# A top-1 expert feed-forward: every expert on every token, or 15 gathered tiles of tokens sorted by expert

## The reference, cut to what matters

```python
scores = feats @ centroids.T                      # 1024 x 8
expert = argmax(scores)                           # one expert for each token
alpha = sigmoid(max(scores))
h = layernorm(feats) * gamma[e] + beta[e]         # a second layernorm
ys[e] = feats + relu(h @ W1[e].T + b1[e]) @ W2[e].T + b2[e]
out = alpha * ys[expert] + (1 - alpha) * feats    # = feats + alpha * (relu(...) @ W2.T + b2)
```

## Time and profile before

| | before |
|---|---|
| median of 3 runs | 762.81 us (762.22 to 766.0) |
| the profiled execution's own time | 763.13 us |
| its span | 761.3 us |
| busy: TensorE, VectorE, ScalarE, GpSimd | 700.4, 524.7, 413.2, 237.6 us |
| mean granted TensorE clock, of full | 0.964 |
| chain that ended last, by engine | TensorE 67%, VectorE 15%, issue 6% |

### The profile page before, as it was taken

One profiled execution on the slowest core, in us unless ns is written; L12 is line 12 of the kernel. 1 busy time (PEld: TensorE's weight loads), 2 busy tenths in 40 slices (PEclk: granted clock), 3 DMA queues, 4 the chain that ended last, 5 costly groups with the idle time before them and its releaser, 6 DMA issues.

```text
span 761.3 us, 13863 instructions
## 1 busy us (share of the span) xinstructions
PE 700.4 (92%) x5137; PEld 511.9 (67%) x5137; DVE 524.7 (69%) x1063; ACT 413.2 (54%) x636; POOL 237.6 (31%) x207
## 2 busy tenths in 40 slices
PE   5999888999999999999998999888999998979995
PEld 4655555665666778777777755476667766748884
DVE  6688676687766648688887588888656556724444
ACT  4387552236665550699995277746665553224442
POOL 4000011014364561022223000013575757046742
PEclk9999899999999998699999999999999999779998
DMA  8200000050013020000024500000022020211112
GB/s 341 122 2 1 2 0 1 0 235 2 26 33 86 2 56 1 1 1 0 0 80 158 226 2 1 2 1 2 1 58 60 26 57 1 57 28 34 43 31 89
DMA packets 9760, 35.54 MB, mean 47 GB/s; under 512 B 1535, under 2 KB 5987, under 8 KB 8162
## 3 DMA queue, kind: packets, MB, share of 16 engines
q1 hardware_dynamic: 7170, 31.58, 12.4%
q0 software_dynamic: 1472, 2.59, 1.6%
q10 hardware_dynamic: 1056, 0.52, 0.2%
HBM read 31.94 MB, written 3.20 MB: 46 GB/s over the span
## 4 chain that ended last, share of the span: by engine, by line
PE 67%; DVE 15%; issue 6%; POOL 5%; ACT 5%; DMA 1%; POOLq 0%; SPq 0%; ACTq 0%; DVEq 0%
PE banks L215 7%; PE banks L216 6%; PE banks L217 6%; PE banks L980 5%; PE banks L487 4%; PE banks L545 4%; PE banks L968 3%; PE banks L2026 3%; PE banks L1017 3%; POOL work L1165 3%; DVE work L772 2%; PE banks L1498 2%; PE banks L2016 2%; PE banks L462 2%; PE banks L504 2%
## 5 line engine op out<-in xcount | busy, mean ns | idle before, releaser
L1165 POOL TENSOR_TENSOR work<-work 128x512 f32<-128x512 f32 x64 | 85.4, 1340 | 95.3 <-ACT work L1127 95.2
L772 DVE TENSOR_REDUCE work<-banks 128x2 f32<-128x512 f32 x128 | 84.5, 688 | 24.2 <-PE banks L487 17.8
L304 POOL TENSOR_TENSOR ln_rstd<-ln_var_eps,minus_half_and_newton 128x4 f32<-128x4 f32 x16 | 17.1, 1066 | 165.0 <-DVE ln_var_eps L270 156.3
L980 PE MATMUL banks<-work 128*64 128x256 f32 x512 | 63.9, 388 | 2.6 <-ACT work L1127 2.2
L1810 DVE TENSOR_TENSOR work_split<-work,work_split 128x512 fp32r<-128x512 f32 x64 | 52.0, 814 | 19.1 <-ACT work_split L1732 18.5
L215 PE MATMUL banks<-normed_t_high,work_split 128*128 128x512 f32 x114 | 55.2, 484 | 4.7 <-DVE normed_t_low L353 2.4
L968 PEld LDWEIGHTS banks<-work_split 64*128 64x128 f32 x768 | 47.6, 186 | 12.6 <-issue 7.2
L968 PE MATMUL banks<-work_split 64*128 64x256 f32 x768 | 54.1, 287 | 0.2
L980 PEld LDWEIGHTS banks<-work 128*64 128x64 f32 x512 | 32.9, 136 | 30.2 <-ACT work L1127 13.8
L1227 DVE TENSOR_TENSOR work_split<-banks,work_split 128x512 fp32r<-128x512 f32 x32 | 21.9, 686 | 44.9 <-ACT work_split L1107 44.8
L1127 ACT ACTIVATE work<-work,small_operands 128x1024 f32<-128x1024 f32 x32 | 36.8, 1150 | 28.6 <-DVE work L1239 28.1
(11 more groups left out here) (360 smaller groups left out, 1777.7 us busy)
## 6 DMA issues: line engine op xcount, KB each, us to landing
raw_b<-in_wf SPq DMA_DIRECT2D x1, 6528.0 KB, 19.0
raw_a<-in_wf SPq DMA_DIRECT2D x1, 4096.0 KB, 12.6
raw_b<-reciprocal_rows SPq DMA_DIRECT2D x6, 512.0 KB, 5.5
raw_a<-reciprocal_rows SPq DMA_DIRECT2D x6, 512.0 KB, 5.5
raw_a<-in_wf SPq DMA_DIRECT2D x1, 2048.0 KB, 14.4
raw_b<-in_wb SPq DMA_DIRECT2D x1, 2048.0 KB, 18.8
raw_a<-in_wb SPq DMA_DIRECT2D x1, 2048.0 KB, 8.3
small_operands<-in_small SPq DMA_DIRECT2D x1, 1386.0 KB, 10.2
```

The costliest lines, as they stand in the source:

```text
L772: nc.vector.tensor_reduce(a_nm[:, t:t + 2, j], bank(7 - n % 2).rearrange("p (e k) -> p e k", e=2), AX.X, ALU.max, negate=True).then_inc(A[ ...
L980: last = nc.tensor.matmul(ps[DH * h:DH * (h + 1), 4, (b % 2) * S:(b % 2 + 1) * S], w_v[:, 2 * b + kb, (2 * p + h) * DH:(2 * p + h + 1) * D ...
L1165: nc.gpsimd.tensor_tensor(w_ps[g % 2].rearrange("p (h q) -> p h q", h=2), v[:, :, 0, :], v[:, :, 1, :], ALU.add).then_inc(W["ps"].sem, 1)
```

## The change

The f1 sublayer is rewritten on the pattern of the last one. VectorE computes factors for the second layernorm exactly, ScalarE writes rows (normed token, alpha, index), SP stores them to HBM, and after ranks and slots 15 tiles of 128 slots are gathered (8 + 7, since each expert may leave one tile partly filled; all 15 are always computed). A tile: transpose, a copy scaled by gamma on VectorE, one native f32 matmul of 512 columns on unsplit weights, a copy out of PSUM on VectorE, four transposes, four activations on ScalarE with the bias at an address held in a register, a one-row product that brings b2, four native f32 products, the factor alpha, a scatter. Then SP loads the 1024 rows back, and VectorE adds them (`f1_add`). Register tables of addresses are loaded by `find` on TensorE, ScalarE and VectorE for eight tiles at a time. The pieces, the clears and the copy to `xh` ahead of the sublayer go; SP's later loads of weights now stand behind `f1_rows`; the last feed-forward shares semaphores and small tensors with this one and is otherwise the same. `rank_products`, `first_of_equals` and `expert_starts` are its lines L2036 to L2039, L2197 to L2198 and L2213 to L2218 moved into functions. The diff, cut:

```diff
- G = signals("f1", E // 2, w=10, up=16, a=16, al=16, dn=16, cb=2, cc=2, t=4, acc=4)
+ TILES1 = NT + E - 1
+ TABLE1 = 2 * NT
  s_gb, s_gd = sem("f1_bias_product"), sem("f1_bias_shifted")
- g_w = [(wr[:, 2048 * s:2048 * s + 1024], wr[:, 2048 * s + 1024:2048 * s + 2048]) for s in range(2)]
...
+ rows1_dram = nc.dram_tensor("token_rows", (T + 1, SLOT), F32, kind="Internal").ap()
+ back1_dram = nc.dram_tensor("expert_tokens", (T, D), F32, kind="Internal").ap()
...
+ M = {n: Count("sorted_" + n, t) for n, t in dict(
+     xs=TILES1, xh=0, xl=TILES1, up=TILES1, sg=0, af=TILES1, tr=TILES1, at=TILES1, o=TILES1, y=TILES1).items()}
...
+ slots1 = wf[:, 0:TILES1 * SLOT].rearrange("p (j c) -> p j c", c=SLOT)
+ rows1 = wf[:, 2048:2048 + NT * SLOT].rearrange("p (t c) -> p t c", t=NT)
+ again1 = wf[:, 2048:2048 + T].rearrange("p (t d) -> p t d", t=NT)
+ n_af = [wf[:, 3200 + 512 * k:3712 + 512 * k] for k in range(2)]
+ n_at = [wf[:, 4224 + 512 * k:4736 + 512 * k] for k in range(2)]
...
+ def find(tables, j, tiles, engine, groups):
...
+     for k, (at, most) in groups.items():
+         _, values = nc.values_load_multi_w_load_instructions(
+             tab_t[0:1, at + j:at + j + n], engines=[engine], min_val=0, max_val=most,
...
+         for i in range(n):
+             tables[j + i, k] = values[i]
...
- def f1_shifts_dve(dve):
+ def f1_shifts_dve(dve, order):
      dve.wait_ge(s_gb, 2)
      b1 = col("b1")
      nc.vector.tensor_tensor(b1, b1, ps[:, 5, S:S + E * NF], ALU.add).then_inc(s_gd, 1)
+     nc.vector.tensor_scalar(n_v2, Z[0].mv[:, :, 1], 1.0 + EPS, EPS * EPS, ALU.mult, ALU.add).then_inc(s_v2, 1)
+     order.done(nc.vector.memset(n_ec[:, 0:1], -63.5))
...
+ def f1_pe(pe, m):
+     def at(name, n):
+         M[name].wait(pe, 0, n)
+     where = {}
+     def slot_back(j):
+         loaded_slot(pe, 0, j)
+         at("xl", j)
+         nc.tensor.transpose(ps[:, 7, 0:P], slots1[:, j, 0:D], ident).then_inc(M["xs"].sem, 1)
+     def up(j):
+         find(where, j, TILES1, mybir.EngineType.PE, {
+             "raw": (0, (E - 1) * W_F1), "b2": (2 * TABLE1, (E - 1) * D)})
+         at("af", j - 1)
+         at("xl", j + 1)
+         nc.tensor.matmul(bank(j % 2), n_x[j % 2], raw_a[:, bass.ds(where[j, "raw"], 512)], start=True, stop=True)\
+             .then_inc(M["up"].sem, 1)
+     def turn(j):
+         at("af", j + 1)
+         at("at", j)
+         for f in range(NF):
+             last = nc.tensor.transpose(ps[:, 4, f * P:(f + 1) * P], n_af[j % 2][:, f * P:(f + 1) * P], ident)
+         last.then_inc(M["tr"].sem, 1)
+     def output(j):
+         at("at", j + 1)
+         at("y", j - 1)
+         o = ps[:, 6 - j % 2, 0:D]
+         nc.tensor.matmul(o, const("ones")[0:1, :], sm[0:1, bass.ds(where[j, "b2"] + SMALL["b2rows"][0], D)],
+                          start=True, stop=False)
+         for f in range(NF):
+             last = nc.tensor.matmul(o, n_at[j % 2][:, f * P:(f + 1) * P],
+                                     raw_a[:, bass.ds(where[j, "raw"] + (512 + f * P), P)], start=False, stop=f == NF - 1)
+         last.then_inc(M["o"].sem, 1)
+     logits_pe(xf, col("centroids"), 5, ready=2 * m + 1)
+     stream(8, 4)
+     rank_products(pe, 0)
+     stream(16, 4)
+     pe.wait_ge(s_spots, 1)
+     for t in range(NT):
+         last = nc.tensor.matmul(ps[:, 7, 256:256 + TABLE1], n_spot[:, t, :], n_b[:, t, :], start=t == 0, stop=t == NT - 1)
+     last.then_inc(s_who, 1)
+     stream(8, 4)
+     pe.wait_ge(s_tab, 5)
+     slot_back(0)
+     slot_back(1)
+     up(0)
+     for j in range(TILES1):
+         if j + 2 < TILES1:
+             slot_back(j + 2)
+         if j + 1 < TILES1:
+             up(j + 1)
+         turn(j)
+         if j:
+             output(j - 1)
+     output(TILES1 - 1)
...
+ def f1_act(act):
+     def at(name, n):
+         M[name].wait(act, 0, n)
+     where = {}
+     def hidden(j):
+         find(where, j, TILES1, mybir.EngineType.Activation, {"b1": (3 * TABLE1, (E - 1) * NF)})
+         at("tr", j + 1)
+         at("o", j - 1)
+         for f in range(NF):
+             ins = nc.scalar.activation(n_at[j % 2][:, f * P:(f + 1) * P], ps[:, 4, f * P:(f + 1) * P], ACT.Relu,
+                                        bias=sm[:, bass.ds(where[j, "b1"] + (SMALL["b1"][0] + f), 1)])
+         ins.then_inc(M["at"].sem, 1)
+     act.wait_ge(s_s2, 1)
+     for t in range(NT):
+         nc.scalar.activation(rows1[:, t, 0:D], xn[:, t, :], ACT.Copy, scale=n_t2[:, t:t + 1]).then_inc(s_row2, 1)
+     act.wait_ge(s_lx, 2)
+     nc.scalar.activation(n_ex, mcol, ACT.Exp, scale=-1.0).then_inc(s_le, 1)
+     act.wait_ge(s_gd, 1)
+     act.wait_ge(s_tab, 5)
+     for j in range(TILES1):
+         hidden(j)
...
+ def f1_pool(pool):
+     nc.gpsimd.iota(idx_t[:, :], pattern=[[P, 2 * NT]], base=0, channel_multiplier=1).then_inc(s_index, 1)
+     pool.wait_ge(s_v2, 1)
+     nc.gpsimd.tensor_tensor(n_r2, n_v2, small_cols[:, 0:1].to_broadcast((P, NT)), ALU.pow).then_inc(s_r2, 1)
+     pool.wait_ge(s_index, 1)
+     nc.gpsimd.tensor_copy(rows1[:, :, D + 1].bitcast(I32), idx_t[:, 0:NT]).then_inc(s_index, 1)
+     pool.wait_ge(s_got, 1)
+     pool.wait_ge(s_rows, 16)
+     pool.wait_ge(s_blanked, 32)
+     def fetch(j):
+         nc.gpsimd.indirect_dma_start(
+             out=slots1[:, j, :], out_offset=None, in_=rows1_dram,
+             in_offset=bass.IndirectOffsetOnAxis(ap=who_t[:, j:j + 1], axis=0), bounds_check=T, oob_is_err=False)\
+             .then_inc(s_slot[j % AHEAD], 16)
+     for j in range(AHEAD):
+         fetch(j)
+     for j in range(TILES1):
+         M["y"].wait(pool, 0, j + 1)
+         nc.gpsimd.indirect_dma_start(
+             out=back1_dram, out_offset=bass.IndirectOffsetOnAxis(ap=slots1[:, j, D + 1:D + 2].bitcast(I32), axis=0),
+             in_=slots1[:, j, 0:D], in_offset=None, bounds_check=T - 1, oob_is_err=False).then_inc(s_back, 16)
+         if j + AHEAD < TILES1:
+             fetch(j + AHEAD)
+     pool.wait_ge(s_back, 16 * TILES1)
+ def f1_rows(sp):
+     sp.wait_ge(s_row2, NT)
+     sp.wait_ge(s_index, 2)
+     sp.wait_ge(s_wrow, 1)
+     sp.dma_start(rows1_dram[1:1 + T, :].rearrange("(t p) c -> p t c", p=P), rows1).then_inc(s_rows, 16)
+     sp.wait_ge(s_rows, 16)
+     sp.wait_ge(s_back, 16 * TILES1)
+     for h in range(2):
+         src = back1_dram[h * HALF:(h + 1) * HALF, :].rearrange("(t p) d -> p t d", p=P)
+         sp.dma_start(again1[:, 4 * h:4 * h + 4, :], src).then_inc(s_again[h], 16)
...
+     def second_factors():
+         dve.wait_ge(s_r2, 1)
+         dve.wait_ge(s_v2, 1)
...
+         nc.vector.tensor_tensor(n_t2, n_t2, n_r2, ALU.mult).then_inc(s_s2, 1)
+     def choose():
+         dve.wait_ge(ld["route"], 16)
+         nc.vector.tensor_reduce(mcol, logits, AX.X, ALU.max).then_inc(s_lx, 1)
+         dve.wait_ge(s_lx, 2)
+         order.step(nc.vector.tensor_tensor(t1, logits, across(mcol), ALU.is_equal))
+         first_of_equals(order, m2col)
+         order.step(nc.vector.tensor_tensor(hot, t1, across(m2col), ALU.is_equal))
+         nc.vector.tensor_tensor_scan(prefix, const("seg"), hot_et, 0.0, ALU.mult, ALU.add).then_inc(s_hot, 1)
+     def row_weights():
+         order.step(nc.vector.tensor_scalar(n_ex, n_ex, 1.0, None, ALU.add))
+         nc.vector.reciprocal(rows1[:, :, D], n_ex).then_inc(s_wrow, 1)
+     def place():
+         dve.wait_ge(s_rank, 1)
+         rank = expert_starts(order, n_ct, n_in, n_ec)
...
+         nc.vector.tensor_tensor(n_spot, const("iota").unsqueeze(1).to_broadcast((P, NT, P)),
+                                 across(n_ss, P), ALU.is_equal).then_inc(s_spots, 1)
+     def table():
+         order.step(nc.vector.tensor_tensor(n_le, n_in.unsqueeze(1).to_broadcast((P, TABLE1, E)),
+                                            across(const("tile_at")[:, 0:TABLE1]), ALU.is_le))
+         order.step(nc.vector.tensor_reduce(n_te, n_le, AX.X, ALU.add))
+         for k, width in enumerate((W_F1, 512, D, NF, 1)):
+             nc.vector.tensor_scalar(tab_t[:, k * TABLE1:(k + 1) * TABLE1], n_te, float(E - 1), float(width),
+                                     ALU.min, ALU.mult).then_inc(s_tab, 1)
+     def who():
+         dve.wait_ge(s_who, 1)
+         nc.vector.tensor_copy(who_t[:, 0:TABLE1], ps[:, 7, 256:256 + TABLE1]).then_inc(s_got, 1)
+     def slot(j):
+         find(where, j, TILES1, mybir.EngineType.DVE, {"gamma": (4 * TABLE1, E - 1)})
+         at("xs", j + 1)
+         at("up", j - 1)
+         nc.vector.tensor_scalar(n_x[j % 2], ps[:, 7, 0:P], gamma_at(where, j), None, ALU.mult).then_inc(M["xl"].sem, 1)
+     def evict(j):
+         at("up", j + 1)
+         at("tr", j - 1)
+         nc.vector.tensor_copy(n_af[j % 2], bank(j % 2)).then_inc(M["af"].sem, 1)
+     def out(j):
+         at("o", j + 1)
+         nc.vector.tensor_scalar(slots1[:, j, 0:D], ps[:, 6 - j % 2, 0:D], slots1[:, j, D:D + 1], None, ALU.mult)\
+             .then_inc(M["y"].sem, 1)
+     second_factors()
+     choose()
+     row_weights()
+     place()
+     table()
+     who()
```

(37 more changed lines are left out.)

374 lines of the change are left out of this document (100 added, 274 removed).

## The result

| | before | after |
|---|---|---|
| median of the runs | 764.4 us (4 runs) | 738.4 us (737.02 to 739.36, 4 runs) |
| ratio to before | | 0.9668, 95% interval 0.9628 to 0.9707 |
| the profiled execution's own time, its span | 763.13, 761.3 us | 739.17, 737.4 us |
| busy: TensorE, VectorE, ScalarE, GpSimd | 700.4, 524.7, 413.2, 237.6 us | 665.2, 467.1, 343.6, 244.5 us |
| mean granted TensorE clock, of full | 0.964 | 0.941 |

Faster, by 3.3%: 739.17 us in the profiled execution where 729.6 was forecast.

What follows compares the result with a forecast made beforehand. TensorE was taken to set the pace, its old stage lasting 106.1 us. Head 20.9, loop 38.5, clock 2.5 and tail 7.7 make 69.6, so -36.5, +3 behind: 729 us, range 720 to 740.

Steps and rivals of the forecast that it cites:

- The head: Routing and gather before the first tile's product: 20.9 us, summed from logits, fillings, ranks, slots, rows of slots, gathers and register loads.
- the filling ahead of the slots: In the head, 16 filling products before TensorE's next step after the ranks: 5.0 us taken, between 4.0 and 6.1.
- The loads of 16 registers ahead of the first product: End of the head: register loads behind the second gather, 0.78 us of issue; 1.1 with the transpose.
- the sentence on the one-row product: In each loop tile, the product for b2 was bounded by 0 and 0.22 us; 0.22 was taken.
- The second load of registers: In the loop, TensorE's second load of address registers was to add up to 0.4 us.
- the half clock in mid-loop: Named sign of error: a PEclk of 0.50 in the middle of the tile loop.
- The clock at the loop's head: First tiles: TensorE waits some 4 us for the gather and loses clock; 2.5 us taken, between 0 and 5.4.
- Tail: From the last product through scatter and load back to SBUF: 7.7 us, between 6.7 and 8.65.
- Behind the stage: Normalisation 4 and the small attention begin on a slow TensorE after the idle tail: +3 us, from 0 to 6.
- ScalarE's four activations: Rival: ScalarE paces the loop at 0.60 us per activation, 2.95 us a tile, +6.5 in all: 736 us; chance 0.10.
- the threshold of 4.9 us a tile: Rival: tiles run one after another, some 5.2 us each, 767 us; it decides from 4.9 a tile; chance 0.04.
- the half clock held for one or two tiles, not for 15: Rival: the clock stays at the half level for all tiles, loop costs 38.5 us more, 765 us; chance 0.03.

Runs made afterwards that it cites:

- the identity product: The changed kernel with the second biases brought in by a 128x128 identity against equal rows instead of one row of ones: 730.7 us, ratio 0.9551.

## Why the prediction was right, and where it was off

- *What bounds it*: right. The old stage took 106.1 and 105.5 us, TensorE's, and what was saved in it, 27.4 us, came out of the span but for 1.2 ahead of it and 2.4 behind. The new loop runs at the sum of TensorE's parts.
- *The head*: right in the sum, 20.9 against 21.1, 18.9 and 19.0; the term that moves is the filling ahead of the slots (bounds 4.0 to 6.1, taken as 5.0, measured 5.46 mostly at the half clock, 3.79 at the full one, where VectorE's slots end 0.3 us later). The store of rows held nothing up. The loads of 16 registers ahead of the first product were on the path as forecast: 0.61 us of issue in the chain after VectorE had the tile ready, 0.78 forecast.
- *The loop: the step that failed is the sentence on the one-row product*, "bounded by 0 and the 0.22 of one of the four products". It is 0.61, above the upper bound, since it also changes the price of its neighbours: 0.22 for the columns, 0.19 and 0.20 for the two changes of row count. 15 x 0.39 = 5.9 us. The upper bound was taken from a product of 128 rows, when the trace held products of 32 among products of 128, with the 0.19 to 0.20 behind them; the nearest row was the one with few rows, not the one with the same columns. The other terms of the tile (0.86, 0.44, 0.89, 0.11) came out exact, as the identity product shows.
- *The second load of registers*, "adds up to 0.4", is the other term that was too small: TensorE stood still 1.36 us, and then ran at the half clock for 3.5 to 7 us. The prediction names no row for the 0.4. The trace of before has a stop of 0.45 us at such a load (724.08 to 724.53), but there two loads of 1.07 and 1.10 us lie under 2.0 us of products, here under 1.1. Together stop and half clock cost 3.2 to 4.9 us over three tiles; the half clock in mid-loop, which the prediction named as a sign of being wrong, was no term of the sum, and its cause is not settled.
- *The clock at the loop's head*: right in place, smaller in size as far as filling shows it: it brought 1.2 us of the 2.5 back.
- *Tail*: 7.7 against 8.0. *Behind the stage*: the span behind the addition is 351.0, 346.5 and 351.1 us after, 348.6 and 351.3 before, so that +3 is not shown; the forecast's reason, fills at the half clock, is in the trace (24 records in 5.4 us), but the executions differ by more.
- *The rivals*: ScalarE's four activations take 1.14 us a tile and pace nothing; the tiles overlap (the threshold of 4.9 us a tile, given for them, is 5.0 by its own sum); the half clock held for one or two tiles, not for 15. The rule of the Trainium skill on a burst after a wait, cited in the prediction ("TensorE: Matmul & The Clock Gate", section on HAM oscillation), agrees with the loop's head in this trace (0.57 from 325 to 333 us) and with the stretch behind the tail (0.51 from 386 to 394 us).
- *Luck*: 738.4 lies within 720 to 740 although the loop took 8.6 us more than forecast. The upper end was made of other things, clock, gather, filling and tail, that hardly came; it held the loop's two errors by its width and not by its reasons.

## What to carry to other kernels

A small product is priced with its neighbours: a one-row product between products of 128 rows cost 0.61 us a tile where a full product of the same columns cost 0.22, so a bias is better brought in by the identity against equal rows. Register loads at tile boundaries are better spread over the tiles, since those of eight tiles at once stopped TensorE for 0.8 to 1.9 us, and those of one tile not visibly; in the time that is shown only together with the identity product. And a forecast for a kernel whose clock moves needs a second profile of before: here the stretch ahead of the change came out at 306.6 and 309.3 us.

## What was not expected of the hardware

A change in the number of rows between two products cost 0.19 to 0.20 us each way at the full clock, with the weight loads standing still for 0.12 to 0.17 us there. The granted clock fell to its lower level for 3.4 us (a mean of 0.83 over 10 us) while TensorE was busy 10.00 of the 10, in the kernel before as in the kernel after. And a stop of 1.4 us was followed by the half clock in three of three profiles of one kernel, while stops of 1.2 and 1.9 us in kernels with another form or number of one product kept 1.00; whether the place of the stop in the loop decides is open.
